# First feed-forward of a two-layer model: FP4 weights kept as exact values, their scales applied on the way out of PSUM

## The reference, cut to what matters

```python
def _L0_ffn_ref(x, gate_up_packed, gate_up_scales, down_packed, down_scales):
    w_gu = _dequant_fp4(gate_up_packed, gate_up_scales, 128)   # value of the code * scale of its group
    w_down = _dequant_fp4(down_packed, down_scales, 128)
    gate_up = jnp.einsum('bsh,oh->bso', x, w_gu)               # h = 512, o = 2 * 1408
    gate, up = (gate_up[..., :I], gate_up[..., I:])
    h = jax.nn.silu(gate) * up
    y = jnp.einsum('bsi,hi->bsh', h, w_down)
    rms = jnp.sqrt(jnp.mean(y * y, axis=-1, keepdims=True) + EPS)
    return y / rms
```

## Time and profile before

| | |
|---|---|
| median of 3 runs (lowest, highest) | 2807.95 us (2807.46, 2809.75) |
| the profiled execution: its own time / its span | 2810.49 / 2808.7 us |
| PE busy in the span, mean granted clock | 92%, 0.96 |
| DVE, ACT, POOL busy in the span | 60%, 46%, 31% |
| layer-0 attention | from the start to 506 us |
| layer-0 feed-forward | 506 to 918 us |

### The profile page before, as it was taken

How to read it: one execution, slowest core, us unless ns; L and a number is a source line. 1 busy time by engine, 2 the same in 40 slices (tenths; PEclk the granted TensorE clock), 3 DMA queues, 4 the chain that set the end, 5 groups by cost and what they waited for, 6 DMA issues and landing times. The chain is left out here.

```text
span 2808.7 us, 48664 instructions
## 1 busy us (share of the span) xinstructions
PE 2588.1 (92%) x17291; PEld 2092.4 (74%) x17291; DVE 1695.8 (60%) x3810; ACT 1291.5 (46%) x3417; POOL 857.5 (31%) x852
## 2 busy tenths in 40 slices
PE   7899987699999799999899999999999998199994
PEld 5666664589999688888688888888888887155552
DVE  6767688744444666666676676666667664722221
ACT  4777777222222444444565555555555554022221
POOL 3344321100000455555322222222222221045552
PEclk9999999799999899999899999999999998599997
DMA  3110021300011555555821431341142128599997
GB/s 135 50 46 23 18 73 46 120 21 31 16 53 53 165 192 194 181 183 182 275 61 40 157 91 54 95 128 46 42 140 69 39 68 242 177 284 306 300 300 144
DMA packets 227278, 340.06 MB, mean 121 GB/s; under 512 B 24800, under 2 KB 111200, under 8 KB 226528
## 3 DMA queue, kind: packets, MB, share of 16 engines
q1 hardware_dynamic: 209728, 293.56, 33.1%
q0 software_dynamic: 14912, 39.85, 6.3%
q10 hardware_dynamic: 2400, 3.55, 0.4%
HBM read 230.56 MB, written 110.53 MB: 121 GB/s over the span
## 5 line engine op out<-in xcount | busy, mean ns | idle before, releaser
L2069 POOL TENSOR_SCALAR a_prob<-a_prob,a_rinv 128x640 f32<-128x640 f32 (+3 forms) x256 | 253.5, 990 | 741.0 <-DVE a_rinv L2231 741.0
L2221 DVE TENSOR_REDUCE a_mx<-a_s_ps 128x1 f32<-128x640 f32 (+3 forms) x256 | 262.2, 1024 | 248.6 <-PE a_s_ps L2141 242.6
L2093 ACT ACTIVATE a_probT<-a_t_ps 128x512 fp32r<-128x512 f32 (+3 forms) x512 | 237.2, 516 | 348.0 <-PE a_t_ps L2149 348.0
L2237 DVE TENSOR_TENSOR a_probT<-a_t_ps,a_probT 128x512 fp32r<-128x512 f32 (+3 forms) x512 | 276.6, 582 | 44.5 <-ACT a_probT L2093 43.7
L2084 ACT ACTIVATE a_prob<-a_s_ps,a_nb,a_rs 128x640 f32<-128x640 f32 (+3 forms) x256 | 268.0, 1047 | 9.3 <-DVE a_nb L2222 9.3
L137 PE MATMUL a_o_ps<-a_probT,a_v 128*128 128x256 f32 x832 | 244.4, 294 | 0.0
L138 PE MATMUL a_o_ps<-a_probT,a_v 128*128 128x256 f32 x832 | 232.7, 280 | 0.0
L139 PE MATMUL a_o_ps<-a_probT,a_v 128*128 128x256 f32 x832 | 232.3, 279 | 0.0
L2149 PE MATMUL a_t_ps<-kept_ident,a_prob 128*128 128x128 f32 x1664 | 224.8, 273 | 2.1 <-POOL a_prob L2069 2.1
L2149 PEld LDWEIGHTS a_t_ps<-kept_ident,a_prob 128*128 128x128 f32 x1664 | 194.1, 141 | 25.0 <-POOL a_prob L2069 2.6
L736 PEld LDWEIGHTS a_bank<-kept_ident,a_prob 128*128 128x128 f32 x1024 | 113.7, 144 | 122.8 <-ACT a_prob L580 92.9
(11 more groups left out here) (307 smaller groups left out, 7100.9 us busy)
## 6 DMA issues: line engine op xcount, KB each, us to landing
expert_ring<-in_w_gate SPq DMA_DIRECT2D x64, 384.0 KB, 17.5
expert_ring<-in_w_up SPq DMA_DIRECT2D x64, 384.0 KB, 19.3
expert_ring<-in_w_down SPq DMA_DIRECT2D x64, 384.0 KB, 22.9
l_q_hi<-p_turned SPq DMA_DIRECT2D x64, 256.0 KB, 2.4
l_q_lo<-p_turned SPq DMA_DIRECT2D x64, 256.0 KB, 2.1
h_split<-l_q_hi SPq DMA_DIRECT2D x62, 256.0 KB, 3.2
h_split<-l_q_lo SPq DMA_DIRECT2D x62, 256.0 KB, 3.8
l_v_hi<-p_vs SPq DMA_DIRECT2D x32, 256.0 KB, 2.2
```

Source lines behind the costliest of these rows:

```text
L2069: pool.tensor_scalar(prob[:, k % 4, 0:w], prob[:, k % 4, 0:w], rinv[:, k % 4:k % 4 + 1], 1.0, ALU.mult, ALU.mult).then_inc(s["weighted"], 1)
L2093: act.activation(probT[0][:, pair % 2, i * 4:i * 4 + n, k % 2], t_ps[i][:, 0:n * P].rearrange("p (m n) -> p m n", n=P), ACT.Copy).then_inc ...
L2221: step(dve.tensor_reduce(mx[:, k % 4:k % 4 + 1], s_ps[:, k % 2, 0:w], AX.X, ALU.max))
L2237: dve.tensor_tensor(probT[1][:, pair % 2, i * 4:i * 4 + n, k % 2], t_ps[i][:, 0:n * P].rearrange("p (m n) -> p m n", n=P), probT[0][:, pai ...
```

## The change

1. **Two passes for gate and up.** The code values of FP4 (0, 0.5, ... 6) are exact in fp32r, so a weight without its scale has no low part. The weight is value only, and each product is two passes (value * low x, value * high x). The scale belongs to a group of 128 inputs and one output; outputs lie on the partitions, so it is a number per partition, and is applied when the product of one group leaves PSUM. So each of the 4 groups x 2 halves has a bank of its own (banks 0 to 3, in turn; jobs `r` = 0 to 7 of a step).
2. **Units of 4 tiles** (512 columns): 4 units x 11 blocks = 44 steps `k`.
3. **Sums outside PSUM.** ACT writes scale * bank into an SBUF tile (r even), DVE does scale * bank + that tile (r odd). Thus two half-sums per half, `total` and `second`, which POOL adds.
4. **A step later.** tanh, silu and split of step k-1 follow the evictions of step k on ACT and DVE; the low part is now made by POOL; `down` of step k-2 follows `up` of step k on PE, with the 4 output tiles in banks 4 to 7 for the whole unit (order: block outside, tile inside).
5. **All 12 gate/up pieces in the attention**, from group 42 on: shift and mask in one group, one multiplication by a constant (into fp32r) in the next; no scale, no ACT copy, no subtraction. Their words are loaded from after group 39 on. Only the down pieces are still scaled and split, piece 0 begun in the drain, the rest in unit 0.
6. The gate/up scales (88 rows of 128) are loaded once, widened and turned by PE at the start of the stage. Layer-norm statistics of the first 4 tiles move into the attention's drain; in the stage they are made for 4 tiles at steps 6 and 7 of a unit, and applied at step 8.
7. The output tiles are first copied from PSUM (2 on ACT, 2 on DVE, step 1), then squared (ACT, step 2), averaged (step 3) and added (steps 3 and 4). In the last unit the tail runs from PSUM, tile by tile. Row loads and stores are of 4 tiles (1 MB) instead of 2.

```diff
-PIECES_AT = GROUPS0 - 15
+BITS_AT = {42: 0, 44: 1, 46: 2, 48: 3, 50: 4, 51: 5, 53: 6, 54: 7, 56: 8, 57: 9, 59: 10, 60: 11}
...
-SUB = 2
+SUB = 4
+BLOCKS0 = ((1, 2), (3, 2), (0, 1), (5, 2), (7, 2), (9, 2))
+LAG0 = 2
+RING_H0 = 3
...
-    def split_low(eng, n):
+    def value_bits(dve, n):
+        dve.tensor_scalar(values(n), bits(n).bitcast(F32), 2.0 ** 126, None, ALU.mult).then_inc(s["valued"], 1)
...
+DOWN_SCALE_AT = {0: (1, 2), 2: (3,), 5: (4,), 8: (5,)}
+DOWN_BITS_AT = {1: 3, 4: 4, 7: 5}
+DOWN_HIGH_AT = {0: 1, 1: 2, 3: 3, 6: 4, 9: 5}
+DOWN_LOW_AT = {3: 2, 6: 3, 9: 4, 10: 5}
...
             def _(pool):
+                def add(k, half):
+                    by, nth = rank["g", k, KC * half + 3]
+                    pool.wait_ge(free[by], nth)
+                    a = total[:, k % 3, half]
+                    pool.tensor_tensor(a, a, second[:, k % 2, half], ALU.add).then_inc(s["summed"], 1)
...
+                for k in range(1, STEPS0 + 1):
+                    u, i = k // IC, k % IC
+                    if k >= 2:
+                        low(k - 2)
+                    add(k - 1, 0)
+                    add(k - 1, 1)
...
             def _(act):
+                for k in range(STEPS0):
+                    for r in (0, 2, 4, 6):
+                        evict(k, r)      # activation(to, bank, Copy, scale=group_scale(k, r))
+                    for job in turned_behind(k):
+                        turned_high(*job)
+                    if k:
+                        tanh(k - 1)
+                    if u and i == 1:
+                        copy_y(u - 1, 0)
+                        copy_y(u - 1, 1)
+                    if u and i == 2:
+                        for t in range(SUB):
+                            square(u - 1, t)
+                    if k:
+                        high(k - 1)
...
             def _(pe):
+                        pe.matmul(bank_of(job)[:], w, xT[u % 2][1][:, a], start=True, stop=False)
+                        pe.matmul(bank_of(job)[:], w, xT[u % 2][0][:, a], start=False, stop=True).then_inc(s["job_done"], 1)
...
+                for k in range(STEPS0):
+                    up(k)
+                    for job in turned_behind(k):
+                        turn(*job)
+                    down(k - LAG0)
+                down(STEPS0 - 2)
+                down(STEPS0 - 1)
...
             def _(dve):
+                def evict(k, r):
+                    dve.wait_ge(s["job_done"], number[job])
+                    job_freed(dve, ("g", k, r - 1))
+                    dve.scalar_tensor_tensor(to, bank_of(job)[:], group_scale(k, r), to, ALU.mult, ALU.add).then_inc(s["free_dve"], 1)
...
+                for k in range(STEPS0):
+                    for r in (1, 3, 5, 7):
+                        evict(k, r)
+                    for job in turned_behind(k):
+                        turned_low(*job)
                     if k:
+                        make(k - 1)
...
+                    if k in DOWN_LOW_AT:
+                        ffn["down_low"](dve, DOWN_LOW_AT[k])
+                    if u and i in (3, 4):
+                        add(u - 1, (2 * (i - 3), 2 * (i - 3) + 1), lambda t: yx[:, t])
...
+                        if i == 8:
+                            dve.wait_ge(h["s"]["rstd_ready"], u + 2)
+                            for t in range(SUB):
+                                normalise(u + 1, t)
```

More of the change, by code:

```diff
@@ new lines, with turned_behind, product_tables @@
+DOWN_SCALE_AT = {0: (1, 2), 2: (3,), 5: (4,), 8: (5,)}
+DOWN_BITS_AT = {1: 3, 4: 4, 7: 5}
+DOWN_HIGH_AT = {0: 1, 1: 2, 3: 3, 6: 4, 9: 5}
+DOWN_LOW_AT = {3: 2, 6: 3, 9: 4, 10: 5}
+def turned_behind(k):
+    u, i = k // IC, k % IC
+    return [(u + 1, 2 * TURN_STEPS.index(i) + t) for t in range(2)] if i in TURN_STEPS and u + 1 < UNITS else []
+def product_tables():
+    order = [("x", 0, t) for t in range(SUB)]
+    for k in range(STEPS0):
+        order += [("g", k, r) for r in range(2 * KC)] + [("x", u, t) for u, t in turned_behind(k)]
+    number, rank, count = {}, {}, {"act": 0, "dve": 0}
+    for n, job in enumerate(order):
+        by = "act" if job[0] == "g" and job[2] % 2 == 0 else "dve"
+        count[by] += 1
+        number[job], rank[job] = n + 1, (by, count[by])
+    return order, number, rank
@@ L1170, in layer0_ffn @@
+        s = {n: sem(n) for n in names.split()}
+        free = {"act": s["free_act"], "dve": s["free_dve"]}
         loaded = h["loaded"]
@@ new lines, in evict @@
+                def evict(k, r):
+                    job = ("g", k, r)
+                    to = (total[:, k % 3], second[:, k % 2])[r // 2 % 2][:, r // KC]
+                    if r == 0 and k >= 3:
+                        act.wait_ge(s["h_made"], k - 2)
+                    if r % KC == 2 and k >= 2:
+                        act.wait_ge(s["summed"], 2 * k - 3 + r // KC)
+                    act.wait_ge(s["job_done"], number[job])
+                    act.activation(to, bank_of(job)[:], ACT.Copy, scale=group_scale(k, r)).then_inc(s["free_act"], 1)
@@ new lines, in copy_y, with mean, add @@
+                def copy_y(u, t):
+                    dve.wait_ge(s["downed"], SUB * (u * IC + IC - 1) + t + 1)
+                    dve.tensor_copy(yx[:, t], y_ps[t][:]).then_inc(s["y_dve"], 1)
+                def mean(n, at, squares):
+                    dve.wait_ge(s["squared"], squares)
+                    dve.tensor_scalar(ms[:, at], ss[:, at], 1.0 / D, RMS_EPS, ALU.mult, ALU.add).then_inc(s["ms_ready"], 1)
+                def add(u, tiles, of):
+                    for t in tiles:
+                        step(dve.scalar_tensor_tensor(x[u % 2][:, t], of(t), rg[:, t:t + 1], x[u % 2][:, t], ALU.mult, ALU.add))
@@ L1425, in layer0_ffn @@
+                make(STEPS0 - 1)
+                nxt["low"](dve, 2)
+                for t in range(SUB):
+                    mean(UNITS - 1 + t, slice(t, t + 1), (UNITS - 1) * SUB + t + 1)
+                    dve.wait_ge(s["rms_ready"], UNITS + t)
+                    step(dve.tensor_scalar(rg[:, t:t + 1], rr[:, t:t + 1], gate[:], None, ALU.mult))
+                    add(UNITS - 1, (t,), lambda t: y_ps[t][:])
+                dve.sem_inc(s["x_ready"], 1)
         st.sems += list(h["s"].values())
```

676 lines of the change are left out of this document (322 added, 354 removed).

## The result

After the change the kernel takes 2763.20 us (median of 4 runs, 2759.97 to 2765.72), against 2808.85 of the kernel before in the same session: ratio 0.9832, 95% interval 0.981 to 0.9853, so 1.7% faster, some 46 us. The profiled execution took 2759.97 us (span 2757.9) where the one before took 2810.49: 50.5 us less. The forecast was 2733.4 (range 2710 to 2768), with 2735.9 for the profiled execution: faster for the reason given, but the median lies 29.8 us above the forecast, near the slow end of its range. Profile against profile 24.1 us of the 74.6 expected did not come; only these can be traced.

What follows compares the result with a forecast made beforehand. PE was taken to bound the feed-forward: 292.3 us of work, 22 stalls, 6 clock, 3.8 and 5.8 end, head -0.7, make 329.2 for 403.8, a gain of 74.6; hence 2733.4 us, range 2710 to 2768.

Steps and rivals of the forecast that it cites:

- PE's work: Feed-forward stage: gate/up 164.3, down 123.2 and transposes 4.8 us, in all 292.3 us, 6.53 us a step.
- Rival 4: Feed-forward steps: DVE's evictions also wait for POOL, 9.6 us a step, 34 us slower, 2842 us; chance 0.05.
- Rival 1: Feed-forward stage: POOL's operations fall between DVE's bursts, stalls 8 us, gain 89, 2719 us; chance 0.17.
- Rival 2: Feed-forward stage: PE, often stalled a little, gets clock 0.83 throughout, gain 37, 2771 us; chance 0.12.
- Rival 5: Feed-forward steps: a bank comes back later than counted; 0.2 us per step is 9 us, inside the range; no chance given.
- Bursts in units 1 and 2: DVE and ACT bursts at steps 2, 3, 4 and 8 overdraw the slack, about 4.3 us a unit.
- Unit 0: First feed-forward unit: down pieces add 13.8 us of DVE work, some 13 us of stalls, most at steps 6 to 8.
- Unit 3 and the end: Last unit: 5 us for two chunks of the next stage's weights; end 3.8 plus 5.8 us after PE's work.
- Drain: End of the attention: statistics (3.8 us) fall into DVE's wait for exp, taken as 0.
- Next stage: Stage after the feed-forward: added waits on stores hold up nothing urgent, taken as 0.
- Attention: Groups 42 to 63: added shifts, masks and multiplications against removed pieces, net 0, range -6 to +8 us.
- rival 3: Attention from group 42: shift-and-mask between copies delays turning, 8 + 6 us, groups of 7 us or more, 2748 us; chance 0.1.

Runs made afterwards that it cites:

- e6: Changed kernel with only PE's order altered: the fourth tile's down matmuls kept back to between the next step's fourth and fifth job; 2757.2 us, ratio 0.9801.
- e1: Changed kernel with a third matmul in every gate and up product, the low product done twice; 2815.8 us, ratio 1.0012.
- the control: The changed kernel run once more, unaltered, beside the kernel before; 2763.8 us, ratio 0.9825.
- e7: Changed kernel with POOL's two additions per step cut to 8 of 512 columns, so the result is not the model's; 2746.3 us, ratio 0.9766.
- e9: Changed kernel with DVE's shifts and scalings of unit 0's down pieces cut to 8 columns, result not the model's; 2757.4 us, ratio 0.9799.
- e12: Kernel of e11 with ACT's first-tile square a step earlier and two down pieces' low parts moved from DVE to POOL; 2738.9 us, ratio 0.9737.
- e10: Changed kernel with e2's earlier words, e4's split normalisations and the next stage's weights made in four halves in the last unit; 2740.4 us, ratio 0.9744.
- e2: Changed kernel with the words of the last three gate and up pieces loaded inside the attention's groups; 2754.7 us, ratio 0.98.
- e11: Kernel of e10 with the last unit's rows stored in two halves of 512 KB, the first earlier; 2737.4 us, ratio 0.9736.
- e4: Changed kernel with the next unit's four normalisations split, two at step 8 and two at step 9; 2750.5 us, ratio 0.978.

## Why the prediction was right, and where its sizes were off

- **PE's work, 292.3 us: right.** Distances of 0.233 us, ordinary steps of 6.53 us as soon as nothing stops them (e6), 8.40 with a third pass (e1). It carried the forecast.
- **The size of the gain: too large by 29.8 us, near the edge of the range.** The terms taken as 0 (drain, next stage) and the stalls and the clock all erred the same way; the range held since it was made of all bad ends together.
- **Rival 4, the lock in every step: out.** Evictions take 0.75 us beside POOL, and e1 could not have filled 27.6 us of waits otherwise.
- **Rival 1, stalls absorbed: out.** Bursts did meet POOL (four normalisations 3.85 us, not 2.2), and the stops are above the forecast's, not below.
- **Rival 2, the clock throughout: out, but the term was too small.** Units 1 and 2 ran at 1.00 in the mean. The clock fell where PE had waited for some time: 0.81 in 0:1, 0.86 in 0:9, 0.73 in 3:6, 0.85 at the end. With its end unit 3 stands at 0.93, under the 0.95 that the forecast named as this rival's sign. In all that is up to 11 us, where 6 (3 to 9) were taken; the forecast expected it in unit 0, and about 8 of the 11 are in unit 3 (3 in the control, for which 3:6 ran at 1.00 and the last step at 0.89).
- **Rival 5, the bank: came true at half size.** I had 0.1 to 0.2 us to spare and took 0; it is 0.1 us short in ordinary steps, at most 4.4 us, if all 44 are counted. e6 shows it.
- **Bursts in units 1 and 2, 4.3 us each: near.** They lie 6.8 and 5.6 above their work, of which 1.1 is the bank. The places (after steps 2 to 4 and 8) and the cause (own length and POOL) are as forecast. e7 puts POOL's share at 12 us over the stage.
- **Unit 0: near in sum, mostly the wrong cause.** 13 of stalls and most of 6 for the clock stand against 17.2. But 7.4 of them are steps 0:0 to 0:2, which the forecast counted at PE's pace; steps 0:6 to 0:8, where it put the most, lie 3.1 above their work. Of the down pieces' shifts and scalings on DVE, to which it gave the stalls, e9 found 1.5 us. Their low parts e9 left in; moving two of them to POOL (e12) took 2.0 us from 0:10 and put 2.3 on 0:7.
- **Unit 3 and the end: the terms most undersized.** 5 for the next stage's weights, 10.2 measured above unit 3's work; 9.6 for the end, 16.0 measured. The single steps (3.6 us of waits for the low part, a tail of 5.3) were as counted (3.8, 5.8); what was missed is that the second chunk's low parts, at step 3:9, fall into the last step (waits of 1.04 and 2.14) and leave PE at a mean clock of 0.85 for it. I costed the weights by their DVE time, without the 1.65 us that DVE waits for ACT in front of them and without POOL. Done in halves (e10) the end falls to 23.8, while the stops at 3:6 only spread over 3:5, 3:7 and 3:8.
- **Drain, 0: wrong, 5.0 us.** From the row of group 63 to the first gate/up matmul it is 34.5 us (before 30.1), and 0.7 less was forecast; the groups' gain of 2.1 below and a start 0.7 earlier leave 2.2 of it. The shifts and masks do stand where scale and low part stood, but they need words, and SP loads these behind a store. The forecast looked at the engine's time and not at when the data are loaded. e2 took it away and found 4 to 6.
- **Next stage, 0: wrong, 3.8 us.** "SP waits nothing urgent" was true of the waits and not of the queue: a store of 1 MB is ahead of the tables. e11 and e12 give back about 3 of it up to the second tile.
- **Attention, net 0 (range -6 to +8): near.** +1.5 in groups 42 to 49 (6.7 us a group; rival 3 looked for 7 and more), -3.6 in 49 to 63.

The term that was mis-sized most is the stalls: 22 were taken, some 36 measured. The forecast's own parts do not give 22: 13 for unit 0, 4.3 each for units 1 and 2 and 5 for unit 3 are 26.6, without unit 3's bursts at steps 2 to 4. And the sum lacked the bank (at most 4.4), the down-less steps (7.4) and most of unit 3. The distribution failed as well as the size; the way of finding the bursts, by their length and by what they meet on POOL, held in units 1 and 2.

## What to carry to other kernels

When four banks hand results from PE to two engines, look up for each burst how much of PE's work lies between the job in front of it and the job that needs the first bank again; shifting PE's order inside that span changes nothing (e6), splitting the burst helps where its halves find room (e4; in e10 at the end of the stage, while in steps 3:5 to 3:9 the stops only spread). Work moved from one engine to another must be followed to its data: which queue loads it, behind which store. And the beginning and end of a pipelined loop, where half of a step's work is missing, are to be counted apart: here they cost 7.4 and 16.0 us above PE's work where a unit in the middle cost 5.6 to 6.8.
